# Layer 0 attention: modulation in two parts, and queries and keys sent through DRAM by halves of the heads

## The reference, cut to what matters

```
mod = (silu(c) @ wmod).reshape(4, 6, 1, 256);  sa, ca, ga, sb, cb, gb = mod[:, 0..5]
ga, gb = sign(g) * max(|g|, 0.25)
h = layernorm(x) * (1 + ca) + sa
x = x + ga * attention(h)
h = layernorm(x) * (1 + cb) + sb
x = x + gb * mixture_of_experts(h)
```

## Time and profile before

| what | value |
|---|---|
| median of 3 runs | 1694.08 us (1686.86 to 1697.18) |
| the profiled execution | 1692.63 us, of which the traced span is 1691.3 us |
| first scores of attention0 | 70.74 us after the span's start |
| attention0 | about 0 to 390 us |
| PE, DVE, ACT, POOL busy | 82%, 55%, 48%, 25% of the span |

### The profile page before, as it was taken

The page is one execution under the profiler, slowest core; times in us unless marked ns, Lnnn a source line. Parts: engine busy times, 40 slices in busy tenths (PEclk is TensorE's granted clock), DMA queues, the critical chain, the costliest instruction groups (busy, mean ns, idle before and its releaser), DMA issues. The chain is left out here.

```text
span 1691.3 us, 23275 instructions
## 1 busy us (share of the span) xinstructions
PE 1381.0 (82%) x6461; PEld 935.0 (55%) x6461; DVE 927.1 (55%) x2799; ACT 804.9 (48%) x1900; POOL 430.4 (25%) x503
## 2 busy tenths in 40 slices
PE   5398898976969984799989998999995644999980
PEld 5143443324545663667767776778874433555550
DVE  2477777615654335555665666567655772333337
ACT  2266566533424322656656665666654331444440
POOL 3343443210446331100000000000000664444443
PEclk9588898757989986899999999999997776999995
DMA  4765744004124331234000000000007222343316
GB/s 141 149 139 102 156 107 74 1 1 184 51 70 150 101 95 54 82 112 126 17 1 1 1 1 1 1 1 1 1 1 296 99 76 87 113 108 110 88 44 248
DMA packets 80298, 134.97 MB, mean 80 GB/s; under 512 B 13980, under 2 KB 52772, under 8 KB 78508
## 3 DMA queue, kind: packets, MB, share of 16 engines
q1 hardware_dynamic: 62000, 92.56, 18.2%
q0 software_dynamic: 15200, 38.25, 8.5%
q10 hardware_dynamic: 2976, 2.69, 0.5%
HBM read 75.53 MB, written 62.63 MB: 82 GB/s over the span
## 5 line engine op out<-in xcount | busy, mean ns | idle before, releaser
L694 DVE TENSOR_REDUCE a_nmax<-psum 128x2 f32<-128x1024 f32 x128 | 155.1, 1219 | 89.0 <-PE psum L682 88.3
L773 ACT ACTIVATE a_et<-psum 128x512 f32<-128x512 f32 x256 | 139.2, 595 | 102.4 <-PE psum L758 100.2
L2130 POOL DMA_INDIRECT results<-r_ys,r_to x134 | 130.5, 974 | 193.7 <-ACT r_ys L2122 182.4
L1313 ACT ACTIVATE a_spare<-psum,a_nmax 128x128 f32<-128x128 f32 (+3 forms) x256 | 134.6, 526 | 92.3 <-DVE a_nmax L1302 90.6
L1360 PE MATMUL psum<-a_et,a_v 128*128 128x512 f32 (+3 forms) x512 | 170.7, 436 | 0.0
L2064 PE MATMUL psum<-m_w,m_xT 128*128 x536 | 166.9, 435 | 3.7 <-ACT m_xT L2047 1.7
L1302 DVE CUSTOM_DVE_ANT_0 psum<-psum,a_spare 128x128 f32<-128x128 f32 (+3 forms) x256 | 126.9, 496 | 67.8 <-PE psum L123 67.4
L1340 ACT ACTIVATE a_et<-psum 128x128 f32<-128x128 f32 (+3 forms) x256 | 111.6, 436 | 58.4 <-PE psum L1331 54.4
L2081 DVE TENSOR_TENSOR m_hid<-m_silu,psum 128x128 f32<-128x128 f32 (+1 forms) x134 | 40.4, 302 | 169.7 <-ACT m_silu L2074 167.4
L1931 POOL DMA_INDIRECT slots<-r_rows,r_slot_of x96 | 93.3, 972 | 140.5 <-DVE r_upto L1858 113.6
L121 PE MATMUL psum<-a_kT,a_q 128*128 128x128 f32 (+3 forms) x256 | 120.1, 469 | 9.1 <-ACT a_spare L1313 6.5
(11 more groups left out here) (265 smaller groups left out, 3112.2 us busy)
## 6 DMA issues: line engine op xcount, KB each, us to landing
r_xs<-slots SPq DMA_DIRECT2D x134, 129.0 KB, 2.2
slots<-empty SPq DMA_DIRECT2D x12, 1290.0 KB, 6.3
stacks<-a_qk SPq DMA_DIRECT2D x96, 128.0 KB, 2.4
a_stk<-stacks POOLq DMA_DIRECT2D x32, 384.0 KB, 8.3
m_w<-in_experts SPq DMA_DIRECT2D x16, 768.0 KB, 14.0
l_res<-results SPq DMA_DIRECT2D x16, 512.0 KB, 5.9
m_w<-in_experts SPq DMA_DIRECT2D x4, 1216.0 KB, 14.7
l_res<-results SPq DMA_DIRECT2D x16, 256.0 KB, 3.4
```

Of the source, the lines that this page charges most:

```text
L694: dve.tensor_reduce(nmax[:, G % 2, qt, 2 * p:2 * p + 2], psum[:, n:n + 2, :], AX.X, ALU.max, negate=True).then_inc(s_max.sem, 1)
L773: act.activation(et[:, n % NET, 2 * p + hh, :], psum[:, 4 + hh, :], ACT.Exp).then_inc(s_e.sem, 1)
L1313: act.activation(e[:, u % NE, 0:W], psum[:, n, 0:W], ACT.Exp, bias=nmax[:, u % NE, :], scale=-1.0, accum_out=rsum[:, u % NE, :]).then_inc( ...
L2130: pool.indirect_dma_start(results[:, :], bass.IndirectOffsetOnAxis(ap=to[:, i % NI, 0:1].bitcast(U32), axis=0), ys[:, o, :], None, bounds_ ...
```

## The change

The modulation is cut in two. Its first part (sa and ca: 4 output tiles, 0.5 MB of wmod in two transfers) stays at the start; the second part (8 output tiles, 1 MB in two transfers) is loaded behind all other weights and computed after batch 0's projections, into other buffers. silu(c) waits for c alone and comes first on ACT. The bias product and the split of the output weights also move behind the projections; POOL splits the q, k, v weights before it waits for the small tables. The partitions of q and k are ordered (hh, half of the heads, 8 channels, 4 heads), so that a half is 32 neighbouring partitions; the planes of qk are ordered even hi, odd hi, even lo, odd lo, so that up to four neighbouring ones form one transfer. sync_to writes half 0 first: per q or k now 8 transfers (4 a half, of 32 partitions and 4 or 2 planes: 256 or 128 KB), with a semaphore for each half; gpsimd_stack waits only for its own half. In layer 1, silu(c) moves from combine step 7 to step 0 and wmod comes in two transfers; the mixture's gate waits for its own semaphore value. The diff, cut to its core:

```
-        self.stacks = nc.dram_tensor("stacks", (B, 2, 2, 6, P // 2, S), F32).ap()
+        self.stacks = nc.dram_tensor("stacks", (B, 2, 2, 2, 6, P // 4, S), F32).ap()
...
-def load_modulation(k, l, w):
+def load_modulation(k, l, part, cols, w):
+    sp, ins, loaded = k.sp, k.ins, k.sem(f"dma_mod{l}{part}")
+    if part == 0:
+        sp.dma_start(k.c[:, l], ins[f"c{l}"]).then_inc(k.sem(f"dma_c{l}").sem, 16)
+        k.sem(f"dma_c{l}").up(16)
+    for i in range(KT):
+        sp.dma_start(w[i], ins[f"wmod{l}"][i * P:(i + 1) * P, cols]).then_inc(loaded.sem, 16)
+        loaded.up(16)
+def scalar_conditioning(k, l):
+    act, silu, loaded = k.act, k.sem("act_silu_c"), k.sem(f"dma_c{l}")
+    act.wait_ge(loaded.sem, loaded.n)
+    act.activation(k.silu_c[:, l], k.c[:, l], ACT.Silu).then_inc(silu.sem, 1)
+    k.silu_ready[l] = silu.up()
+def tensor_modulation(k, l, part, outs, w, bank, bank_free):
...
+    pe.wait_ge(loaded.sem, loaded.n)
+    pe.wait_ge(*k.silu_ready[l])
+    for m in outs:
+        c = (m - outs[0]) * P
         for i in range(KT):
+            mm = pe.matmul(ps[:, m, :], w[i][:, c:c + P], k.silu_c[:, l, i, :], start=(i == 0), stop=(i == KT - 1))
+def vector_modulation(k, l, outs, bank, t_mm):
... (the DVE part of modulation(), for the tiles in outs only)
-        wmod = flat[:, 0:KT * 6 * D].rearrange("p (k n) -> p k n", k=KT)
+        wmod = [later[:, i, :] for i in range(KT)], [oT[:, :, :].rearrange("p k s -> p (k s)"),
+                                                     turn_work[:, :, :].rearrange("p k s -> p (k s)")]
+        outs, cols = (range(4), range(4, 12)), (slice(0, 2 * D), slice(2 * D, 6 * D))
...
-        norm.vector_stats(range(TT))
-        norm.scalar_sd()
-        norm.vector_rstd()
-        first = g.next()
-        load_modulation(k, 0, wmod)
-        wmod_read, g.free[first] = modulation(k, 0, wmod, first, None)
-        for j in range(len(staged)):
+        load_modulation(k, 0, 0, cols[0], wmod[0])
+        for j in range(n_w):
             sync_stage(j)
... (rope, small tables, ones)
+        for j in range(n_w, len(staged)):
+            sync_stage(j)
+        load_modulation(k, 0, 1, cols[1], wmod[1])
         load_rest_of_x(k)
... (constants on POOL)
-        pool.wait_ge(*small)
-        pool.tensor_scalar(bias[:, 1:2], bias[:, 1:2], HD0 ** -0.5, None, ALU.mult)...
+        scalar_conditioning(k, 0)
+        norm.vector_stats(range(TT))
+        norm.scalar_sd()
+        norm.vector_rstd()
         (identity rounded on ACT; then, for each of the n_w pieces:)
             scalar_stage(j)
             gpsimd_stage(j)
-        pe.wait_ge(*k.ident_ready)
+        pool.wait_ge(*small)
+        pool.tensor_scalar(bias[:, 1:2], bias[:, 1:2], HD0 ** -0.5, None, ALU.mult)...
...
         def sync_to(b, i):
             sp.wait_ge(*lo_ready[b, i])
-            for x, blocks in enumerate((((0, 1), (2,), (3, 4), (5,)), ((0, 2), (1,), (3, 5), (4,)))[i]):
-                for block in blocks:
+            for half in range(2):
+                for rows, lo, n in (((0, 0, 4), (4, 0, 2)), ((0, 0, 2), (2, 0, 4)))[i]:
                     for hh in range(2):
-                        sp.dma_start(k.stacks[b, i, hh, block],
-                                     qk[64 * hh:64 * hh + 64, i, x, :].bitcast(F32)).then_inc(s_to[i].sem, 16)
-                        written[b, i] = qk_free[i] = s_to[i].up(16)
+                        first = 64 * hh + 32 * half
+                        sp.dma_start(k.stacks[b, i, half, hh, rows:rows + n].rearrange("x r s -> r x s"),
+                                     qk[first:first + 32, i, lo:lo + n, :].bitcast(F32)).then_inc(s_to[i][half].sem, 16)
+                        written[b, i, half] = s_to[i][half].up(16)
+            qk_free[i] = [written[b, i, half] for half in range(2)]
...
         def gpsimd_stack(half, i):
-            pool.wait_ge(*written[b, i])
+            pool.wait_ge(*written[b, i, half % 2])
             for hh in range(2):
-                src = k.stacks[b, i, hh].bitcast(F32R).rearrange("k (i p) s -> (k i) p s", p=2 * HALF0)
-                pool.dma_start(stk[64 * hh:64 * hh + 48, i, slot],
-                               src[:, HALF0 * (half % 2):HALF0 * (half % 2 + 1), :])...
+                src = k.stacks[b, i, half % 2, hh].bitcast(F32R).rearrange("k (i p) s -> (k i) p s", p=HALF0)
+                pool.dma_start(stk[64 * hh:64 * hh + 48, i, slot], src)...
...
+        first = g.next()
+        modulated = tensor_modulation(k, 0, 0, outs[0], wmod[0], first, None)
+        pe.wait_ge(*k.ident_ready)
         for n in range(TT):
             norm.vector_xn(0, n, n)
             norm.tensor_turn(0, n, g)
+            if n == 1:
+                g.free[first] = vector_modulation(k, 0, outs[0], first, modulated)
         norm.vector_h(0, g)
         norm.scalar_hi(0)
         norm.gpsimd_lo(0)
-        bias_at = tensor_bias()
... (q, k, v projections; for i in 0, 1: ropes, halves, sync_to)
-        norm.vector_stats(range(TT, NT), TT)
-        norm.scalar_sd()
-        norm.vector_rstd()
-        vector_bias(*bias_at)
+        for j in range(n_w, len(staged)):
+            scalar_stage(j)
+            gpsimd_stage(j)
         for half in range(2):
             scalar_v(0, half)
         for half in range(2):
             for i in range(2):
                 gpsimd_stack(half, i)
-        for j in range(n_w, len(staged)):
-            scalar_stage(j)
-            gpsimd_stage(j)
+        bias_at = tensor_bias()
+        first = g.next()
+        modulated = tensor_modulation(k, 0, 1, outs[1], wmod[1], first, g.free[first])
+        norm.vector_stats(range(TT, NT), TT)
+        norm.scalar_sd()
+        norm.vector_rstd()
+        vector_bias(*bias_at)
+        g.free[first] = vector_modulation(k, 0, outs[1], first, modulated)
...
-    return np.broadcast_to(table[None, :, None], (2, HD0 // 2, H0 // 2, 3, S)).reshape(P, 3, S)
+    return np.broadcast_to(table[None, None, :, None], (2, 2, HD0 // 2, HALF0, 3, S)).reshape(P, 3, S)
-    place = np.arange(D).reshape(H0 // 2, 2, HD0 // 2, 2).transpose(3, 1, 2, 0).reshape(2, P)
+    place = np.arange(D).reshape(2, HALF0, 2, HD0 // 2, 2).transpose(4, 2, 0, 3, 1).reshape(2, P)
```

More of the change, by code:

```diff
@@ L200, in modulation @@
+def scalar_conditioning(k, l):
+    act, silu, loaded = k.act, k.sem("act_silu_c"), k.sem(f"dma_c{l}")
     act.wait_ge(loaded.sem, loaded.n)
-    act.activation(sc[:, l], c[:, l], ACT.Silu).then_inc(silu.sem, 1)
-    silu_c = silu.up()
+    act.activation(k.silu_c[:, l], k.c[:, l], ACT.Silu).then_inc(silu.sem, 1)
+    k.silu_ready[l] = silu.up()
+def tensor_modulation(k, l, part, outs, w, bank, bank_free):
+    pe, loaded, done = k.pe, k.sem(f"dma_mod{l}{part}"), k.sem("pe_mod")
     if bank_free:
@@ L205, in modulation @@
         pe.wait_ge(*bank_free)
-    pe.wait_ge(*silu_c)
+    pe.wait_ge(loaded.sem, loaded.n)
+    pe.wait_ge(*k.silu_ready[l])
     ps = k.psum[:, bank, 0:12 * B].rearrange("p (m b) -> p m b", b=B)
-    for m in range(12):
+    for m in outs:
+        c = (m - outs[0]) * P
         for i in range(KT):
-            mm = pe.matmul(ps[:, m, :], w[:, i, m * P:(m + 1) * P], sc[:, l, i, :], start=(i == 0),
-                           stop=(i == KT - 1))
+            mm = pe.matmul(ps[:, m, :], w[i][:, c:c + P], k.silu_c[:, l, i, :], start=(i == 0), stop=(i == KT - 1))
@@ L236, in modulation @@
-    return t_mm, bank_read
+    for which, j in enumerate((1, 4)):
+        if 2 * j in outs:
+            v = mod[:, 2 * j:2 * j + 2, :]
+            dve.tensor_scalar(v, v, 1.0, None, ALU.add).then_inc(vec.sem, 1)
+            k.mod_ready[l, which] = vec.up()
+    for n, j in enumerate((2, 5)):
+        if 2 * j in outs:
+            g = mod[:, 2 * j:2 * j + 2, :]
+            neg, sign, mag = (k.gate_work[:, l, i, n] for i in range(3))
+            dve.tensor_scalar(neg, g, -1.0, None, ALU.mult).then_inc(vec.sem, 1)
+            vec.up()
+            dve.tensor_scalar(sign, g, 0.0, 2.0, ALU.is_ge, ALU.mult).then_inc(vec.sem, 1)
+            dve.wait_ge(*vec.up())
+            dve.tensor_tensor(mag, g, neg, ALU.max).then_inc(vec.sem, 1)
+            dve.wait_ge(*vec.up())
+            dve.tensor_scalar(neg, mag, 0.25, None, ALU.max).then_inc(vec.sem, 1)
+            dve.wait_ge(*vec.up())
+            dve.scalar_tensor_tensor(k.gate[l][:, n], sign, -1.0, neg, ALU.add, ALU.mult).then_inc(vec.sem, 1)
+            k.gate_ready[l, n] = vec.up()
@@ L326, in vector_h @@
             dve.wait_ge(*free)
-        dve.wait_ge(*k.mod_ready[self.l])
+        dve.wait_ge(*k.mod_ready[self.l, self.which])
         dve.wait_ge(*self.turned[b])
@@ L590, in scalar_halves @@
         def scalar_halves(b, i):
-            if qk_free[i]:
-                act.wait_ge(*qk_free[i])
+            for free in qk_free[i]:
+                act.wait_ge(*free)
             act.wait_ge(*o_ready[b, i])
-            act.activation(qk[:, i, 2, :], turned(b, i)[:, 1, :], ACT.Copy).then_inc(s_qkhi.sem, 1)
```

(9 more changed lines are left out.)

71 lines of the change are left out of this document (25 added, 46 removed).

## The result

The changed kernel took **1668.82 us** (median of 4 runs, 1663.08 to 1671.13) against 1690.47 for the kernel before (4 runs, 1675.08 to 1697.18): ratio 0.9878, 95% interval 0.9841 to 0.9914. The forecast was 1672, in a range of 1661 to 1683. A second set of runs, six of the changed kernel against eleven of before, gave 1662.91 and 1690.22, ratio 0.9856 (0.9814 to 0.9898). The profiled execution took 1669.87 us, with a span of 1668.5, so profile against profile the change is -22.8 us where the sum said -20.5.

What follows compares the result with a forecast made beforehand. Attention0 was taken as bound by the stk round trip before first scores at 70.7 us, by PE after. -14.5 - 5.6 - 1.4 = -21.5, 1 us given back, from 1692.63: 1672 us, range 1661 to 1683.

Steps and rivals of the forecast that it cites:

- The place: Before the first scores at 70.7 us: every microsecond taken off there moves all that follows.
- Part 1: Start up to the first write: smaller modulation and earlier loads start the projections at about 19.3 instead of 33.8, -14.5 us.
- late bound of 23: Latest projection start allowed, in us, with POOL free only at 20.4, a gain of 11 us.
- Part 2: Round trip of q and k from first write to first scores: 21.9 instead of 27.5 us, -5.6, bounds -2.5 and -8.
- 9.5: Us for the 12 writes ahead of k's first load, taken between issue-bound 7.4 and bandwidth-bound 11.5.
- The rule set beside part 2: Port swizzle: 32 or 64 partitions reach 8 of 16 ports, about 218 GB/s; alone, 10.8 us for 2.36 MB.
- Cover: Work moved behind the projections hides beside the round trip: price zero, with 6 us of cover.
- Part 3: Later batches: POOL's wait for k's writes at batch 1 goes, -1.4 us; batch 2 and layer 1 unchanged.
- (a): Rival: transfers limit the writes, late tables the start; projections at 23, round trip 25, -13.5, 1679 us; chance 0.20.
- (b): Rival: the stalls at batch boundaries vanish together with their slow clock stretches, -28.4, 1664 us; chance 0.12.
- (c): Rival: the clock stays low longer; 50 us more eat the gain, 90 us more give 1710 us; chance 0.04.
- 140 us at the lower level: Time attention0 behind 70.7 us was said to spend at the lower clock: 0.36 x 389 us, each costing 0.43.

Runs made afterwards that it cites:

- e1: The changed kernel's prologue (split modulation, its load order) with the writes, waits and head order of the kernel before; 1673.19 us, ratio 0.9909.
- e2: The kernel before with only the new round trip: new head and plane order, 8 transfers per q or k, a semaphore per half; 1680.86 us, ratio 0.9954.
- e5: The changed kernel with the two loads of ones issued after POOL's low part of h instead of first; 1677.08 us, ratio 0.9859.
- e7: The changed kernel, but in batch 0 POOL loads q's first half only once k's half 0 is written too; 1667.84 us, ratio 0.9805.
- e4: The changed kernel with the old head order, no halves, 4 transfers of 64 partitions per q or k, loads waiting for all of them; 1665.27 us.
- e3: The changed kernel with its new writes, but each load of stk waits for the writes of both halves; 1667.47 us.
- e9: The changed kernel with each half's four writes ordered so that two in a row lie in the same 64 partitions; 1662.84 us, one run.
- e6: The changed kernel with the matmuls of the modulation's second part done twice; 1665.71 us, ratio 0.9792.
- e8: The changed kernel with POOL's loads of the next batch's first half put ahead of its other work in their step; 1672.28 us, ratio 0.9819.

## Why the prediction was right, and where a step was off

**The place.** That the wait at the first scores is worth its full length held: 20.5 us taken there are 22.8 us of the whole. e1 and e2 show the same, less cleanly: 13.8 and 5.6 us there, 16.9 and 9.3 between the medians. How near the total came is in part luck: the medians of the first set are 21.7 us apart, those of the second 27.3.

**Part 1, -14.5.** Right in size (-14.3) and in its last link, POOL's chain w_lo, bias, h_lo. Right for a reason only half named: the identity's lateness, which carried the late bound of 23, did not occur (9.03), and the tables' landing, forecast for 16 and seen at 16.2, was not the limit. The weights were, at 12.33, and e5 shows what held them up; the forecast's 12 was scaled from a rate and met the number without that cause.

**Part 2, -5.6.** Right within the trip's own spread (-3.9 to -6.8), and its terms came out near their size: 9.5 + 1.8 = 11.3 us for the writes of q and of k's half 0 by themselves (11.0 in e7), 3.1 for q's loads beside them (2.3 to 5.1), 7.5 for the load (7.3 to 8.0). The 9.5, though, was chosen between an issue cost of 0.62 us and a limit of 205 GB/s without a row that could tell them apart. The trace of before can. Its SP issues (L616) from 43 to 52.8 us:

```profile
L616 SPq DMA_DIRECT2D stacks<-a_qk x15: 494/597/701, 43.2 to 52.2; - x15
...
DMA to landing us min/median/max: 2.3/2.4/2.6
```

Fifteen writes followed each other at 0.60 us an issue in the median, and all landed 2.3 to 2.6 us after their issue: nothing piled up behind the transfers. The next nine landed beside q's loads, 5.1 to 7.2 us after their issue, and SP still took 0.60 to 0.62 us for each of them but the last (1.92). So SP's issue paced the old writes. In the new trip neither is the bound: SP took 0.45 us in the median for one of the 64 writes. The twelve that k's half 0 waits for were issued in 7.8 us, no less than twelve of the old ones but with half again the bytes; that was by 36.59, 5.6 us before POOL saw them landed, and the transfers reached 316 GB/s. And the forecast put the gain on waiting for three quarters of the bytes: e4 gets 23.0 us while waiting for all of them. Merging is enough there; with the 32-partition transfers of the change the wait for a half is needed (e3).

**The rule set beside part 2.** It would have kept 2.36 MB at 10.8 us. Slices of 285 to 316 GB/s by the writes alone are above the about 218 GB/s that the Trainium skill, "SBUF — State Buffer", section on the DMA port swizzle, gives for transfers of this kind one after the other. Here the measurement decides: queued transfers together did go faster than that. That it is the two halves of the partitions that overlap is argued, not shown; e9 shows only that their order is not what does it. The agreement that the forecast saw, 205 GB/s before, was one of numbers: that pace was SP's. Whether transfers of that form could have gone faster is not shown, as the engines were 80 to 90% busy at it.

**Cover, -0.** Held, by e6 also when the work is doubled. The forecast had batch 1 transposed 15.7 us after the first write; it was 11.3 (40.14), as the bias product took 1.84 us instead of 3.41 and the first 22 of the 32 records of the second modulation started 0.11 us apart.

**Part 3, -1.4.** POOL's wait at batch 1 went as forecast and PE's stall there with 2.4 of its 3.76 us. But attention0 behind the first scores differs by only 0.8 us, and the step that failed is the free credit for it. Behind the first scores PE's waits for stk fell from 7.9 to 5.7 us (23.8 less 15.9, 14.7 less 9.0), while its waits for the rows of maxima rose from 1.8 to 4.9. The groups of 40 to 370 us, before and then changed:

```profile
L758 PE MATMUL psum<-a_stk 50*128 50x512 f32 x256 | 114.7, 532 | 11.3 <-ACT a_et L773 9.2 <-DMA a_stk<-a_nrow 1.8
```

```profile
L772 PE MATMUL psum<-a_stk 50*128 50x512 f32 x256 | 113.4, 517 | 14.6 <-ACT a_et L787 9.6 <-DMA a_stk<-a_nrow 4.9
```

**The rivals.** (a) no: 19.49 and 21.4, not 23 and 25; the flat 199 to 226 GB/s that it rests on has slices of 156 to 195 in it. (b), that the stalls vanish and take the slow stretches with them, did not occur: at 1.34 us of stall the clock was 0.58. e8 shows that the stalls can be taken away, at a price named nowhere in the forecast: the next wait, for the rows of maxima. (c), the clock eating the gain, did not occur in the compared profiles (0.82 against 0.81), and its price was too high. So were its 140 us at the lower level: that window runs on to 460, and attention0 alone, at 0.81 over 317.36 us, has 121. The fourteen traces run attention0 from the first scores with the same 1380 matmul records in 298.7 to 323.7 us, at a mean grant of 0.90 (or 0.91) to 0.79. Take e4 and e1, one job: (1 - 0.90) x 2 x 298.7 = 60 us at the lower level against (1 - 0.79) x 2 x 323.7 = 136, and 25.1 us between them, 0.33 each; a straight line through all fourteen gives 0.30 to 0.31, not 0.43.

e4 and e1 in windows, first scores to the last addition:

```profile
52.02:350.69 298.67, 259.85 (x1380) 118.77 (x1380) 202.76 (x220) 175.37 (x328) 103.63 (x169) 0.90 0.40 86
```

```profile
56.94:380.67 323.73, 285.11 (x1380) 127.48 (x1380) 203.09 (x220) 175.81 (x328) 103.64 (x169) 0.79 0.39 79
```

This is why, in their traces, e3 and e4 end attention0 no later than the changed kernel though their scores start later: e4's 298.67 against 316.56 is 18 us, with 0.90 against 0.82, and e3's 310.56 is 6, with 0.85. It also moves one kernel against itself: of the eleven runs of before in the last job the fastest, 1676.12 us, had a mean grant of 0.903, and the slowest, 1694.80, one of 0.886. Whether any edit here changes the clock on average, these few runs cannot say; what the clock followed is open.

## What to carry to other kernels

Find the one instruction on which the rest hangs, and account for a change in its start time before you look at the total: here that number was good to 2 us when totals scattered by 10. Compare the granted clock of the stretch behind it before you credit or blame a stage. And when a load or an engine is made earlier, look at what it now falls beside: weights 3.8 us sooner bought nothing until POOL was told to stay off DVE's turn, and loads without a stall raised the next wait from 4.9 to 13.5 us.

## What the runs showed of the hardware

- Two transfers of 2 rows of 24 KB held up the landing of loads queued on another engine's queue: the median time from issue to landing of the q, k, v weights was 10.4 us with them in front and 5.6 without (e5).
- Reading back from DRAM delays writing to it: k's writes were complete after 11.0 us alone (e7) and 13.3 to 16.1 beside q's loads.
- The issue of a write from 64 partitions of 2 KB took SP 0.60 us (before), whether the write landed 2.4 us later or 7.2; issued one behind the other these writes moved 205 GB/s, and fewer, larger ones up to 316.
- DVE instructions wait out a POOL subtraction: a tensor_tensor of 0.16 us became 1.25, two tensor_scalars of together 0.73 became 2.59.
- The same round trip fell into two groups 1.4 us apart (up to 21.4, from 22.8), by whether k's writes or q's loads were done first; what decides that is open.
